# Expert weights split during attention, and expert outputs added to DRAM rows by scatters

## The reference

```
x = x + cross_attention(layernorm(x), ctx)      # 16 heads of 128, q and k normed
x = x + ffn_hadamard(layernorm(x))              # 512 -> 2 x 2048 -> 512
x = x + ssm(ctx, layernorm(x))                  # a scan over 512 steps, 16 states
x = x + moe(layernorm(x))                       # this case's last stages

# moe, for the 2048 rows t and 16 experts e of inner width 256
probs = softmax(xt @ Wr.T + bias);  topk_val, topk_idx = top_k(probs, 2)
w = topk_val / sum(topk_val)
y = (silu(xt @ Wg[e]) * (xt @ Wu[e])) @ Wd[e]   # for the two experts of each row
routed = sum over the two of w * y
shared = (silu(xt @ sWg) * (xt @ sWu)) @ sWd
moe = routed + shared
```

## Time and profile before

| | us |
|---|---|
| median of 3 runs | 2648.81 |
| lowest, highest | 2648.68, 2650.52 |
| span of the profiled execution | 2643.4 |

### The profile page before, as it was taken

How to read it: one execution, slowest core, us unless ns; L and a number is a source line. 1 busy time by engine, 2 the same in 40 slices (tenths; PEclk the granted TensorE clock), 3 DMA queues, 4 the chain that set the end, 5 groups by cost and what they waited for, 6 DMA issues and landing times. The chain is left out here.

```text
span 2643.4 us, 35123 instructions
## 1 busy us (share of the span) xinstructions
PE 2284.0 (86%) x10784; PEld 1760.5 (67%) x10785; DVE 1797.4 (68%) x3239; ACT 1279.1 (48%) x2275; POOL 1356.7 (51%) x1104
## 2 busy tenths in 40 slices
PE   3699999999999999999693899998998869578980
PEld 2688888888887888887442666665665547456770
DVE  6466777768677777876683998898988966312323
ACT  2344454444454444544383866757766632223430
POOL 0232333323333333333293988989979941488324
PEclk8799999999999999999886999999999988789995
DMA  7513232122322232211348565555565321665317
GB/s 286 216 53 113 88 112 79 58 109 89 113 78 79 88 113 89 87 64 39 131 166 265 168 208 204 175 185 187 196 183 183 123 84 48 215 219 173 117 52 266
DMA packets 136761, 363.49 MB, mean 138 GB/s; under 512 B 21264, under 2 KB 58768, under 8 KB 118416
## 3 DMA queue, kind: packets, MB, share of 16 engines
q1 hardware_dynamic: 123504, 328.30, 36.1%
q0 software_dynamic: 6320, 20.71, 2.4%
q10 hardware_dynamic: 6768, 12.32, 1.2%
HBM read 289.99 MB, written 71.30 MB: 137 GB/s over the span
## 5 line engine op out<-in xcount | busy, mean ns | idle before, releaser
L641 POOL TENSOR_SCALAR att_probs<-att_probs,att_recip 128x512 f32<-128x512 f32 x256 | 181.8, 713 | 562.6 <-DVE att_recip L708 562.6
L1819 POOL TENSOR_TENSOR mix_drive<-mix_du,mix_rows 128x512 f32<-128x512 f32 x256 | 326.6, 1282 | 48.8 <-DVE mix_state L1891 15.9
L565 ACT ACTIVATE att_probs<-att_s,att_bias,att_rq 128x512 f32<-128x512 f32 x256 | 200.6, 784 | 288.3 <-DVE att_bias L704 288.1
L1891 DVE TENSOR_TENSOR_SCAN mix_state<-mix_state,mix_drive 128x512 f32<-128x512 f32 x256 | 312.9, 1222 | 30.8 <-POOL mix_drive L1819 17.3
L1671 ACT ACTIVATE mix_state<-mix_delta,mix_a 128x512 f32<-128x512 f32 x256 | 175.8, 690 | 227.8 <-DVE mix_drive L1902 187.4
L1804 POOL TENSOR_TENSOR mix_y<-mix_y,mix_drive 128x512 f32<-128x512 f32 x180 | 230.6, 1281 | 46.0 <-DVE mix_drive L1902 45.8
L1580 PE MATMUL mix_down<-mix_wd,mix_hT 128*128 128x512 f32 x512 | 232.0, 596 | 8.8 <-DVE residual_x L1922 8.8
L703 DVE TENSOR_REDUCE att_nmax<-att_s 128x1 f32<-128x512 f32 x256 | 175.1, 684 | 71.4 <-PE att_s L101 64.6
L744 DVE TENSOR_TENSOR att_pT<-att_pt,att_pT 128x512 fp32r<-128x512 f32 x256 | 170.1, 686 | 66.0 <-ACT att_pT L571 61.9
L571 ACT CAST att_pT<-att_pt 128x512 fp32r<-128x512 f32 x256 | 144.2, 593 | 133.4 <-PE att_pt L422 129.2
L99 PE MATMUL att_w<-att_w_qkv,att_cx 128*128 128x256 f32 x512 | 158.7, 310 | 35.2 <-DVE att_w_qkv L690 26.5
(11 more groups left out here) (354 smaller groups left out, 6703.7 us busy)
## 6 DMA issues: line engine op xcount, KB each, us to landing
att_xn<-normT SPq DMA_DIRECT2D x32, 2048.0 KB, 8.7
mix_gu<-guT SPq DMA_DIRECT2D x64, 1024.0 KB, 8.2
mix_rows<-bc_d SPq DMA_DIRECT2D x128, 256.0 KB, 4.8
guT<-att_ffnT SPq DMA_DIRECT2D x32, 512.0 KB, 5.7
mix_wd<-wdT SPq DMA_DIRECT2D x16, 1024.0 KB, 7.9
slots<-exp_y ACTq DMA_DIRECT2D x47, 256.0 KB
normT<-nrm_outT SPq DMA_DIRECT2D x4, 2048.0 KB, 9.1
exp_raw<-in_L_ffn_Wg SPq DMA_DIRECT2D x16, 512.0 KB, 5.1
```

What stands on the lines that cost most here:

```text
L565: act.activation(probs[:, n, :], ps_s[n % 2][:, :], ACT.Exp, bias=bias[:, n:n + 1], scale=rq[:, n:n + 1], accum_out=sums[:, n:n + 1]).then ...
L641: pool.tensor_scalar(probs[:, n, :], probs[:, n, :], recip[:, n:n + 1], 1.0, ALU.mult, ALU.mult).then_inc(s_pn, 1)
L1819: pool.tensor_tensor(drive[q % RING][:, :], du[i % DUS][:, :], rows[g % ROWS][:, 0, :], ALU.mult).then_inc(s_drive, 1)
L1891: dve.tensor_tensor_scan(h[:, :], h[:, :], drive[q % RING][:, :], 0.0, ALU.mult, ALU.add).then_inc(s_scan, 1)
```

## The change

In words, by stage:

- Attention. `pairs` is now a Python loop, so that all 32 iterations are written out on every engine, VectorE too, and every wait has a constant value. (On GpSimd the extra semaphore step beside each wait, `wait_apart`, is gone.) In each iteration half of one expert's weights (1536 of 3072 columns) is loaded raw into `ew`, split on GpSimd (two instructions) and stored with both parts to DRAM, `split_w`. The contexts are loaded anew in each iteration, into two buffers in place of four.
- Router. The two weights and the two expert numbers of each row are kept as four more columns (`tags`) and stored behind the row in `xrows` (516 columns). `plan.target` is the row to which each slot belongs; an unused slot goes to one of 128 spare rows behind the 2048 in `mixed`.
- Experts. The steps are written out. SyncE loads both parts of an expert's weights in one transfer (3 MB) into a ring of four, each next one when the expert four before it has ended and the load before it has landed. Gathers run eight tiles ahead into ten buffers and TensorE turns the rows from these. VectorE finds the weight of each slot from the tags; ScalarE's copy of the output multiplies by it, into one of four buffers. GpSimd adds the tile to `mixed` in DRAM by an indirect transfer that accumulates. Each waits for the landing of the one before it.
- Combine is gone. When all 47 additions have landed, one transfer copies the 2048 rows of `mixed` to the output.

```diff
         def pairs(eng, iteration):
 
-            with eng.Fori(0, PAIRS - 1) as hp:
+            for hp in range(PAIRS):
                 for b in range(B):
-                    iteration(hp, b, False)
-            for b in range(B):
-                iteration(PAIRS - 1, b, b == B - 1)
+                    iteration(hp, b, hp == PAIRS - 1 and b == B - 1)
...
+                def store_expert(i):
+                    e, half = divmod(i, 2)
+                    sp.wait_ge(s_elo, i + 1)
+                    sp.dma_start(split_w[e][:, :, half * HALF_COLS:(half + 1) * HALF_COLS],
+                                 ew[:, :, :].bitcast(F32)).then_inc(s_est, 16)
...
                 def iteration(hp, b, last):
                     i = hp * B + b
-                    if b == 0 and not (isinstance(hp, int) and hp == PAIRS - 1):
+                    if i + 2 < PAIRS * B:
+                        sp.wait_ge(s_v, 2 * i + 2)
+                        load_ctx(i + 2)
+                    if i:
+                        sp.wait_ge(s_est, 16 * i)
+                        load_expert(i)
+                    if b == 0 and hp < PAIRS - 1:
                         sp.wait_ge(s_w, 2 * hp + 2)
                         load_weights(hp + 1)
...
                     store_ffn(hp, b)
+                    store_expert(i)
...
+                def split_expert(i):
+                    pool.wait_ge(s_ein, 80 * (i // 2) + (32, 80)[i % 2])
+                    raw_w = ew[:, 1, :].bitcast(F32)
+                    pool.tensor_scalar(ew[:, 0, :], raw_w, 1.0, 1.0, ALU.mult, ALU.mult).then_inc(s_ehi, 1)
+                    pool.wait_ge(s_ehi, i + 1)
+                    pool.tensor_tensor(ew[:, 1, :], raw_w, ew[:, 0, :].bitcast(F32), ALU.subtract).then_inc(s_elo, 1)
...
                     if not last:
                         norm_q(j)
+                    split_expert(i)
...
+                sp.wait_ge(s_tags, 1)
+                sp.dma_start(xrows[:, DIM:TAGGED].rearrange("(n p) d -> p n d", p=P), tags[:, :, :],
+                             allow_slow_non_contiguous=True).then_inc(s_tagsout, 16)
...
+                for e in range(WRING):
+                    load(e)
+                for e in range(WRING):
+                    loaded(e)
+                for e in range(WRING, EXPERTS):
+                    end = sp.value_load(plan.ends[0:1, e - WRING:e - WRING + 1], min_val=1, max_val=TILES)
+                    wait_apart(sp, s_y, end, s_pace)
+                    load(e)
+                    loaded(e)
+                sp.wait_ge(s_add, 16 * TILES)
+                sp.dma_start(out, mixed[0:B * S, :]).then_inc(s_out, 16)
+                sp.wait_ge(s_out, 16)
...
+                def add(k):
+                    pool.wait_ge(s_yout, k + 1)
+                    if k:
+                        pool.wait_ge(s_add, 16 * k)
+                    pool.indirect_dma_start(mixed, bass.IndirectOffsetOnAxis(plan.target[:, k:k + 1], 0),
+                                            yout[k % YS][:, :], None, compute_op=ALU.add).then_inc(s_add, 16)
+
+                for k in range(AHEAD):
+                    gather(k)
+                for k in range(TILES):
+                    if k + AHEAD < TILES:
+                        gather(k + AHEAD)
+                    add(k)
...
+                def y_out(k):
+                    act.wait_ge(s_y, k + 1)
+                    act.wait_ge(s_weight, k + 1)
+                    if k >= YS:
+                        act.wait_ge(s_add, 16 * (k - YS + 1))
+                    act.activation(yout[k % YS][:, :], ps_y[k % 2][:, :], ACT.Copy,
+                                   scale=weight[:, k:k + 1]).then_inc(s_yout, 1)
...
-def stage_combine(nc, x, y, out, plan):
```

479 lines of the change are left out of this document (203 added, 276 removed).

## The result

| | before | after |
|---|---|---|
| median of four runs, us | 2649.0 (2648.7 to 2650.5) | 2680.9 (2674.4 to 2684.6) |
| the profiled execution: span, us | 2643.4 | 2678.6 |
| attention: the same GpSimd instruction, first to last iteration, us | 1128.8 | 1150.1 |
| from the first weight load of the experts to the end, us | 372.8 | 387.3 |

The changed kernel is slower: ratio 1.0123, 95% interval 1.0103 to 1.0143. The prediction was 2590 us with a range of 2525 to 2672, so it has the wrong sign and the range misses. Between the two stages named nothing moved (1015.2 and 1015.3 us). The span of the profiled execution grew by 35.2 us (the medians are 31.9 apart): 21.3 in attention, 14.5 in the experts and what follows, and -0.6 elsewhere.

The account below looks back on a forecast made before the run. It took TensorE to bound attention, the chain of scatters the changed experts, and DMA the combine. Span 2643.4 - 24 (attention) - 34.4 (experts and combine) = 2585.0, plus 5.4 around the span: 2590 us, range 2525 to 2672.

Parts of the forecast that it names:

- loops written out: Attention: removing six back edges, at 4 us each between bounds of 17.6 and 27 us in all, gains 24 us.
- expert split in attention: Attention: GpSimd's two added instructions, 5.1 us per iteration, fit in an 11.22 us gap; cost 0, up to 24 us.
- router: Router: five more VectorE instructions and a store of 2048 pieces of 16 bytes; 0 to 1 us, taken as 0.
- first scatter after the stage's start: Experts: about 20 us pass before the first scatter, at about 2291; first product at about 2284.
- first scatter to last landing: Experts: 20 tiles at 8.0 us beside weight loads and 27 at 5.3 us; sum 299 us, last landing at 2590.
- copy to the output: End: one 4 MB copy from DRAM to DRAM replaces combine; 18 us, and 1 us for the end.
- experts and what follows: Experts and combine together: stage ends at 2609 against 2643.4, a gain of 34.4 us.
- quiet price: Experts: one accumulating scatter without weight loads beside it, issue to landing, costs 5.3 us (3.6 + 1.7).
- the cover: Attention: GpSimd's gap of 11.22 us before its next wanted step hides the added split, leaving 6 us of slack.
- Rival 3: Attention: written-out code gives nothing, through code fetches and added transfers on the DMA engines; 24 us stay, 2614 us; chance 0.16.
- a scatter beside weight loads: Experts: one scatter, issue to landing, costs 8.0 us there (6.8 + 1.2, from gathers); ends 4.0 and 10.
- rival 2: Experts: scatters bind everywhere, costing more than combine did; loses above a mean of 7.6 us; at 8.4, 2686 us; chance 0.20.

Follow-up runs that it names:

- e2: The kernel before with only attention's loops written out on all engines: 2625.0 us, ratio 0.9914; attention 1107.3 us.
- e6: Changed kernel without GpSimd's two split instructions (transfers kept), and with adds alternating between two arrays, never merged: attention 1107.7 us, experts 304.6 us.
- e10: Changed kernel with GpSimd waiting for both VectorE weight splits, and two chains of adds to two arrays, merged at the end: 2580.9 us, ratio 0.9756.
- e3: Changed kernel with each 3 MB expert weight load issued as twelve 256 KB transfers with 2 KB rows: 2666.0 us.
- e13: Changed kernel with GpSimd waiting for both VectorE weight splits, each 3 MB load one issue in 512-byte pieces (2 KB meant): 2628.0 us.
- e1: Changed kernel with one more wait: before a pair change GpSimd starts its expert split only after VectorE's attention weight split: 2648.0 us, ratio 0.9992.

## Why the prediction was wrong, point by point

| term | predicted | measured |
|---|---|---|
| loops written out | -24 | -24.7 (e2) |
| expert split in attention | 0, up to +24 | +42.8 (after against e2) |
| router | 0 to 1 | 0.1 |
| first scatter after the stage's start | 20 | 30.4 |
| first scatter to last landing | 299 | 341.0 |
| copy to the output | 19 | 15.9 |
| experts and what follows | -34.4 | +14.5 |

**Right.** Back edges: 4 us each, read from two intervals and bounded by TensorE's stall. The duration of GpSimd's two instructions (5.1 us predicted, 1.48 + 3.51 measured), the gap that they fit in, the transfers hidden behind them (e6), and the end of the stage. That the gain of the removed splits goes into the chain of scatters, its quiet price (5.3 predicted, 5.6 measured) and TensorE's own 5.0 us per tile (5.1 in e10).

**Failed: "I cost it at nothing", the expert split in attention.** I looked for what waits for GpSimd and for room on GpSimd, both rightly, and not for what VectorE does in that gap. The step that failed is the cover: in the earlier trace rows I named the next thing wanted of GpSimd, and in two of four iterations VectorE splits attention's own weights in the same 11 us. The prediction knows of that split (its last paragraph sets one iteration in four apart for it) and puts no price on it. Rival 3 had 24 us for this stage, with code and transfers as its mechanisms; e6 shows that neither is one. The mechanism was not among my cases, and its 42.8 us alone are more than my whole upper bound for the term. Without it the changed kernel would be at 2638, 0.4% faster than before, within my range.

**Mis-sized: a scatter beside weight loads, 8.0 us.** It takes 11.7. I took it from gathers beside the loads of before, whose rows are 1 and 2 KB, and named in rival 2 that a load now moves rows of 24 KB, without letting it into the price. That accounts for a part: with rows of 2 KB a contended step takes 9.4 us (e3) and with 512 bytes 8.8 (e13), so even then it is above 8.0. The loads fill about the time that I gave them, 13 steps of 11.7 or 152 us, where I had 156; but 13 tiles go in it and not 20. The other 33 steps cost 5.6 each, 185 us, where I had 27 at 5.3, 143 us. With 4.5 for the last landing it is 341 and not 299, 42 us more. Rival 2 had a mean over 7.3, and its break-even at 7.6: the mean is 7.31 to the last scatter and 7.26 to the last landing, on the border of what I had given to it.

**Mis-sized: the start, 20 us.** Four loads of 3 MB and nine gathers are issued at once. The first load lands after 10.8 us, as predicted (11 to 13), but the gathers land after 27 us, and TensorE waits 17.3 us for its first rows: the first product starts 17.5 us after the first load, where I had 14 from the stage's start. From there to the first scatter are 12.9 us, where I had 7. TensorE makes the second tile's gate and up ahead of the first's down, and the first tile's products take 0.63 us each where the second's take 0.40. I costed one load and one tile as if they were alone.

## What to carry to other kernels

Work moved to GpSimd is not free because GpSimd is idle: here it cost 42.8 us, by VectorE's copies and two-input instructions in the same gap. Look at both engines' timelines there, in every kind of iteration and not in a steady one. Price a step of a chain through memory by its landing beside the transfers that will be under way then, and not by that of another kernel's smaller ones; here two chains hid what no tuning of the rows did. Read from the trace what a parameter did to the transfers (e13's pieces are a quarter of what I meant). A wait added to an engine can make the kernel faster (e1), when two engines are in each other's way.

## What the runs showed of the hardware

- A VectorE copy of 0.69 us took up to 4.04 and a subtraction of 1.23 up to 4.42 beside GpSimd's instructions; GpSimd's own 3.51 became up to 4.37. In the meeting shown, each VectorE instruction that started second ended about its own length after GpSimd's.
- An indirect store with addition takes GpSimd 1.59 us to issue and 5.6 from one to the next in a quiet chain; without addition 0.99 and 3.5.
- Beside 3 MB loads in rows of 24 or 12 KB a scatter of 128 rows of 2 KB lands after up to 11.7 to 12.6 us; beside rows of 2 KB in twelve issues after up to 9.8 and 10.5, with at most 1 MB of them under way 8.0; beside one issue in pieces of 512 bytes 8.3. The load itself slows from 11.9 us (24 KB) to 14.5 (512 bytes).
- Four issues of 3 MB one after another take SyncE 34.7 us in pieces of 512 bytes and 2.2 in rows of 24 KB; each later one, alone, 0.36 and 0.32.
- A pair of adding scatters to two arrays took 12.3 us beside loads, one alone 11.7.
- TensorE's granted clock in the experts was 0.88 with 249 us busy of 341 (after) and 0.99 with 231 of 252 (e10).
